# Storing the turned tokens in attention and loading them in the shared expert

## The reference

```python
x = x + attention(layernorm(x))
h = layernorm(x)                     # 8 x 1024 x 256
scores = softmax(h @ gate_w.T)       # 16 experts
# each expert takes its 128 best tokens of each sequence:
# out += (gelu(h_e @ Wg.T) * (h_e @ Wu.T)) @ Wd.T * score
shared = (gelu(h @ Ws_g.T) * (h @ Ws_u.T)) @ Ws_d.T
x = x + out + shared
```

## Time and profile before

| | us |
|---|---|
| median of three runs | 2423.66 |
| lowest and highest run | 2422.8, 2426.49 |
| profiled execution, span from first to last instruction | 2427.3 |
| attention, to the barrier | 1530.9 |
| shared expert with its choice of tokens | 1530.9 to 1832.4 |
| experts | 1832.4 to the end |
| PE busy | 2283.2 (94%) |
| DVE, ACT, POOL busy | 1891.8, 1632.3, 886.1 |

### The profile page before, as it was taken

How to read it: one execution, slowest core, us unless ns; L and a number is a source line. 1 busy time by engine, 2 the same in 40 slices (tenths; PEclk the granted TensorE clock), 3 DMA queues, 4 the chain that set the end, 5 groups by cost and what they waited for, 6 DMA issues and landing times. The chain is left out here.

```text
span 2427.3 us, 44076 instructions
## 1 busy us (share of the span) xinstructions
PE 2283.2 (94%) x16398; PEld 1340.3 (55%) x16398; DVE 1891.8 (78%) x3506; ACT 1632.3 (67%) x3168; POOL 886.1 (37%) x1223
## 2 busy tenths in 40 slices
PE   5899999999999999999999988899997999999996
PEld 4233334334334334334333323788886888888886
DVE  5999999999999999999999994466654555555553
ACT  2599999999999999999999987323323343333432
POOL 4051451451451451441542220000003666666664
PEclk8799999999999999999999999799998999999998
DMA  2000011010010010010010010332322545454443
GB/s 76 1 18 1 1 36 36 1 50 22 1 55 17 9 61 3 19 53 1 19 36 1 19 36 18 126 100 78 104 61 81 115 109 112 87 112 113 100 99 35
DMA packets 104364, 122.74 MB, mean 51 GB/s; under 512 B 7553, under 2 KB 91393, under 8 KB 104193
## 3 DMA queue, kind: packets, MB, share of 16 engines
q1 hardware_dynamic: 79616, 86.90, 11.2%
q0 software_dynamic: 24576, 33.57, 8.1%
HBM read 78.50 MB, written 41.94 MB: 50 GB/s over the span
## 5 line engine op out<-in xcount | busy, mean ns | idle before, releaser
L474 DVE TENSOR_REDUCE sb_MX<-ring 128x1 f32<-128x512 f32 x2048 | 1284.5, 681 | 82.0 <-PE ring L782 65.4
L606 ACT ACTIVATE sb_PR<-rot 128x512 f32<-128x512 f32 x2048 | 1123.3, 621 | 102.8 <-PE rot L793 92.3
L782 PE MATMUL ring<-sb_KT,sb_QT 32*128 32x512 bf16 x2048 | 517.1, 390 | 48.9 <-DVE sb_MX L474 36.5
L804 PE MATMUL pv<-sb_PR,sb_VA 128*32 128x512 f32 x4096 | 547.0, 606 | 2.9 <-ACT sb_OT L661 0.6
L782 PEld LDWEIGHTS ring<-sb_KT,sb_QT 32*128 32x128 bf16 x2048 | 128.1, 91 | 632.9 <-DVE sb_MX L474 565.8
L793 PE MATMUL rot<-sb_QT,sb_KT 32*128 32x512 bf16 x2048 | 422.1, 386 | 1.6
L1095 ACT ACTIVATE ex_GL<-ex_gu 128x512 f32<-128x512 f32 x128 | 76.4, 597 | 347.4 <-PE ex_gu L63 345.2
L1162 DVE TENSOR_TENSOR ex_HF<-ex_GL,ex_gu 128x512 f32<-128x512 f32 x128 | 87.5, 684 | 250.8 <-ACT ex_GL L1095 250.8
L1059 POOL DMA_INDIRECT out<-ex_YS,ex_rows_out x128 | 208.8, 1631 | 44.3 <-issue 43.8
L1016 POOL TENSOR_TENSOR ex_pool_scratch<-identity 128x1 f32<-128x1 f32 x96 | 35.1, 366 | 477.6 <-POOLq L859 332.0
L61 PE MATMUL ex_gu<-ex_XH,weights_high 128*128 128x512 f32 x512 | 200.4, 391 | 2.4 <-DVE ex_XL L1154 2.4
(11 more groups left out here) (168 smaller groups left out, 4272.2 us busy)
## 6 DMA issues: line engine op xcount, KB each, us to landing
sb_XA<-x SPq DMA_DIRECT2D x8, 1024.0 KB, 5.5
sb_XR<-x SPq DMA_DIRECT2D x8, 1024.0 KB, 5.8
out<-sb_XR SPq DMA_DIRECT2D x8, 1024.0 KB, 4.5
xn<-sb_XN SPq DMA_DIRECT2D x8, 1024.0 KB, 4.5
sh_XG<-xn SPq DMA_DIRECT2D x16, 512.0 KB, 5.5
sh_X<-out SPq DMA_DIRECT2D x16, 512.0 KB, 4.9
weights<-WgT SPq DMA_DIRECT2D x16, 512.0 KB, 4.0
weights<-WuT SPq DMA_DIRECT2D x16, 512.0 KB, 5.6
```

The lines of the kernel that those rows point to most:

```text
L474: nc.vector.reduce_max(MX[:, unit % 2, half, j, qt % 4:qt % 4 + 1], ring[m % RING][:], AX.X).then_inc(ring_done, 1)
L606: out = nc.scalar.activation(PR[V % P_STEPS][:, j, :], R[:], ACT.Exp, scale=0.25)
L782: nc.tensor.matmul(ring[m % RING][:], QT[g][r, P * qt:P * qt + P], KT[g][r, 512 * half:512 * half + 512], start=True, stop=True, tile_posi ...
L804: out = nc.tensor.matmul(pv_bank[head(j), :], VA[b % 2][:, kt, 4 * g + j, :], PR[V % P_STEPS][:, j, :], start=(kt == 0), stop=(kt == TT - 1))
```

## The change

The turned tokens that attention makes for the gate in `XT` are stored to a new DRAM tensor, `xn2T`, as they lie: for each sequence 256 rows (features) of 1024 tokens. SP does that behind the load of `XR`, after the last `x2t` copy (`store_turned`). ACT's first `aot` copy of each later sequence waits until the store before it has landed, and the end of attention waits for all eight. The shared expert loads 512 columns of those rows straight into `XG`, whose shape is now that of `XH`. ACT and DVE make the high and low parts from `XG` in SBUF, and PE turns no tokens in this stage. The experts stay as they are, and so does the store of `xn2`, which they gather from.

```diff
@@ attention, SP
+            def store_turned(b):
+                sp.wait_ge(rot_done, done(("x2t", b, KH - 1, 1)))
+                sp.dma_start(d["xn2T"][bass.ds(b * H, H), :].rearrange("(k p) t -> p k t", p=P), XT[:]).then_inc(xt2_out, 16)
...
                     sp.wait_ge(xn2_out, 16 * b)
                     sp.dma_start(XR[:], rows("x", b)).then_inc(xr_in, 16)
+                    store_turned(b - 1)
             store_x1(B - 1)
             store_xn2(B - 1)
+            store_turned(B - 1)
+            sp.wait_ge(xt2_out, 16 * B)
@@ attention, ACT, empty
+                    if kind == "aot" and b and h == 0 and half == 0:
+                        act.wait_ge(xt2_out, 16 * b)
@@ feed_forward
-        XG = [sb(f"XG{c}", [P, CT, D], F32) for c in range(2)]
+        XG = [sb(f"XG{c}", [P, KD, N] if shared else [P, CT, D], F32) for c in range(2)]
@@ SP, load
-                        sp.wait_ge(turned_full, n - 1)
-                    sp.dma_start(XG[k % 2][:], rows("xn2", n)).then_inc(x_in[k % 2], 16)
+                        sp.wait_ge(xl_ready, n - 1)
+                    sp.dma_start(XG[k % 2][:], d["xn2T"][bass.ds(r * D, D), N * k:N * k + N].rearrange("(k p) t -> p k t", p=P)
+                                 ).then_inc(x_in[k % 2], 16)
@@ ACT, split_tokens
-                act.wait_ge(turned_full, n + 1)
-                nc.scalar.copy(XH[k % 2][:], turned[:, :, 0:N]).then_inc(xh_ready, 1)
+                if shared:
+                    act.wait_ge(x_in[k % 2], 16 * (r + 1))
+                    if not (isinstance(n, int) and n < 2):
+                        act.wait_ge(gu_full, KF * (n - 1))
+                    nc.scalar.copy(XH[k % 2][:], XG[k % 2][:]).then_inc(xh_ready, 1)
@@ DVE, split_tokens
-                nc.vector.tensor_tensor(XL[k % 2][:], turned[:, :, 0:N], XH[k % 2][:].bitcast(F32),
-                                        ALU.subtract).then_inc(xl_ready, 1)
+                nc.vector.tensor_tensor(XL[k % 2][:], XG[k % 2][:] if shared else turned[:, :, 0:N],
+                                        XH[k % 2][:].bitcast(F32), ALU.subtract).then_inc(xl_ready, 1)
@@ PE
-            turn_tokens(0, 0)
+            if not shared:
+                turn_tokens(0, 0)
...
-                    if not (last and k == K - 1):
+                    if not shared and not (last and k == K - 1):
                         turn_tokens(r if k < K - 1 else r + 1, (k + 1) % K)
@@ program
+    d["xn2T"] = nc.dram_tensor("xn2T", (B * D, 1024), F32, kind="Internal").ap()
```

More of the change, by code:

```diff
@@ L204, in attention @@
         xn2_out = sem("xn2_out")
+        xt2_out = sem("xt2_out")
         wh_ready = sem("wh_ready")
@@ L1089, in split_tokens @@
                 n = r * K + k
-                act.wait_ge(turned_full, n + 1)
-                nc.scalar.copy(XH[k % 2][:], turned[:, :, 0:N]).then_inc(xh_ready, 1)
+                if shared:
[3 more added lines that the diff above has]
+                    nc.scalar.copy(XH[k % 2][:], XG[k % 2][:]).then_inc(xh_ready, 1)
+                else:
+                    act.wait_ge(turned_full, n + 1)
+                    nc.scalar.copy(XH[k % 2][:], turned[:, :, 0:N]).then_inc(xh_ready, 1)
             def gelu(n, f):
```

## The result

The changed kernel took 2411.84 us (median of four runs, 2411.27 to 2413.09). The kernel before, timed beside it, took 2425.07 us. The ratio is 0.9943, with a 95% interval of 0.9928 to 0.9957. The forecast was 2410.6 us and a difference of 13.05; the measured medians lie 13.23 apart. The 1.2 us by which the forecast was low come from the kernel before: its median of three runs had been 2423.66, 1.4 us lower.

What follows compares the result with a forecast made beforehand. PE, busy 94% of the span and all the time inside the shared expert, was taken as the bound. Fifteen turns at 0.87 us, all else 0, gave 2423.66 - 13.05 = 2410.6 us; range 2407.5 to 2414.5 (its own 2408.5 to 2413).

Steps and rivals of the forecast that it cites:

- The term of the sum: Shared expert: fifteen of sixteen turns leave PE's full queue at 0.87 us each, 13.05 us saved.
- The sixteenth turn at nothing: Head of the shared stage: chunk 0's turn is covered by the weights, so removing it gains nothing.
- The swap of sources: Shared expert: making the tokens' high and low parts from SBUF instead of PSUM costs nothing.
- The stores at nothing: Attention: eight 1 MB stores taken at 0, from 0 to 3 us for each of seven; the last lands before the barrier.
- the 8 us in its list of rivals: End of attention: room given as the argument against the eighth store holding the barrier.
- a store that lands before the gate scores are done: End of attention: a sign of a right forecast, the store of turned tokens landing before the gate scores are done.
- the first rival: End of attention: the eighth store holds the barrier, landing 1 to 4 us after 1530.86; 2411.6 to 2414.6 us, chance 0.07.
- The clock: Head of the shared stage: PE's time at the lower clock level changes by up to 0.9 us each way, taken as 0.
- The smaller turn: Shared expert: a turn's room on PE is only 0.65 us, giving 2413.9 us; chance 0.04.
- DVE as the bound: Shared expert: DVE's 0.32 us of room vanish, the step stays at 17.5 us, time about 2423; chance 0.03.
- stores that slow attention: Attention: DMA reads of XT hold up the engines 3 us per store, giving 2431.6 us; chance 0.03.
- more than forecast: Shared stage: the head starts 2 us sooner and the clock rises earlier, giving 2407.7 us; chance 0.03.

Runs made afterwards that it cites:

- e4: Changed kernel with eight transposes put back at the head of the shared stage alone, their result unused; 2415.20 us, ratio 0.9947.
- e1: Kernel before with only the eight stores of turned tokens and their waits added; 2427.00 us, ratio 0.9999.
- e0_changed: The changed kernel as it is, timed again against the kernel before; 2415.76 us, ratio 0.9950.
- e8_changed_again: The changed kernel as it is, timed once more against the kernel before; 2413.21 us, ratio 0.9948.
- e3: Kernel before with each turn of the shared expert done twice, 8 more transposes per chunk; 2439.53 us, ratio 1.0049.
- e7: Changed kernel with one more 128x512 DVE instruction before the fourth product of every chunk but the first; 2422.02 us, ratio 0.9982.
- e6: Changed kernel with the shared stage's head reordered: tokens split before weights, PE starting on the first split weight; 2411.03 us, ratio 0.9935.

## Why the prediction was right

**The term of the sum.** 15 x 0.87 = 13.05 us, against 13.23 between the medians, and 0.88 by the steps of the trace. That the medians agree within 0.2 us is luck: in the later rounds the changed kernel lay 11.4 and 13.6 us below the kernel before. The steps are what shows the term. Both ways of pricing a turn held, the row of PE and the missing turn of the last chunk (0.89). The result also decides against the smaller figure. By the 81 ns of the Trainium skill's page "TensorE: Matmul & The Clock Gate" (section "Back-to-back issue gap") it would have been an estimated 9.7 us. Here the steps with no, one and two turns show 0.109 us for each fp32 transpose.

**The sixteenth turn at nothing.** Right, for the reason given: e4 has it back under the weights.

**The swap of sources.** In the loop ACT's copy takes 1.05 us from SBUF (1.02 from PSUM before) and DVE's subtraction 1.21 us, as before. DVE's idle time in front of the third product shrank by the turn's 0.88 and no more.

**The stores at nothing.** Right in attention, where e1 shows 0.9999 and the units are the same to 0.01 us. At the barrier this term was the weak one, and small. The prediction had the store land by 1528.4 to 1529.2 with the end at 1530.86, 1.7 us or more of room; the 8 us in its list of rivals is the time from issue to barrier, and not room. It asked for a store that lands before the gate scores are done. That held by 2.8 us in e0_changed and by 0.1 in the first trace, and failed in e8_changed_again, where the store cost 0.5 us: less than the 1 to 4 us of the first rival, and nothing that the medians could show. What the prediction took as fixed was the end of attention, which comes up to 5 us sooner in some executions.

**The clock.** The lower level at the head of the shared stage lasted 4.8 us before, 3.6 in the changed kernel's first trace (1537.28 to 1540.83) and 5.3 in e0_changed: within the 0.9 us allowed each way. At the head of the experts it lasted 2.7 us before and in e0_changed, but 5.3 in the changed kernel's first trace, 1.2 us of time, which is more than the prediction allowed. What it left out is that the same play of levels stands at the end of attention, and is larger there: 4.7 us of span. The profiled execution of the kernel before was one that ended attention late. If its timed runs mix early and late ends, that explains the step from span to median (3.6 us down); their spread, 2422.8 to 2429.6 us over all rounds, fits, but only profiled executions show their stages, so it is not shown.

**The rivals.** The smaller turn fell by the steps of e3, DVE as the bound by the step of 16.66, and stores that slow attention by e1 and its unchanged units. The eighth store came true in one trace of the changed kernel, at 0.5 us. DVE as the bound was nearest: 0.60 us of added work in the right place used up its 0.3 us of room and made it true, as e7 shows. The rival "more than forecast" took a head 2 us sooner, for which nothing in the edit stood; another order gives it, as e6 shows, but the change didn't.

## What to carry to other kernels

Price work that is taken off a full engine by looking for a round of the same loop that already lacks it: its step gives the price and shows at once whether the other engines follow. Work on the same engine that lay under the load of the weights was worth nothing here (e4), and the order in which the waiting engines took what landed there was worth two or three microseconds (e6). Count the room of a new transfer from the earliest end of the stage that its execution can have, and not from the one in the profile (e8). Compare steps and stages of two traces before their spans, as the clock can move a span by several microseconds at a place that the change doesn't touch.

## What the runs showed of the hardware beyond what I expected

The clock can come to its upper level on transposes alone. In e3_turn_twice PE did 16 transposes of chunk 0 and 8 of the gate scores at the head of the stage, after 6.3 us without work; by stretch, with the granted clock third from the end:

```profile
1530.00:1532.00 2.00, 1.95 (x9) 1.96 (x10) 0.00 (x0) 0.65 (x1) 0.00 (x0) 0.50 0.99 372
1532.00:1534.00 2.00, 2.00 (x12) 2.00 (x11) 1.23 (x1) 1.17 (x2) 0.00 (x0) 0.50 0.94 307
1534.00:1536.00 2.00, 0.89 (x7) 0.65 (x5) 1.69 (x2) 2.00 (x3) 0.00 (x0) 0.95 1.10 378
```

It then fell again at about 1537.6, after a pause of 1.93 us, in the first up block. So the first three matmuls there ran at the upper level, and the next at the lower, until 1540.97. That is 3.4 us at the lower level, where the other traces show 2.7 to 5.7 at this place: one trace can't say that extra turns there gain anything.

And a halted PE pays for its restart: 0.11 us between its first two matmuls on top of the wait (e7), fourteen times in the stage.
